# New orders on four engines in the attention rounds of a gated attention and expert block, and slots kept in PSUM

## The reference, cut to what matters

```
x = x + tanh(g0) * attn(layernorm(x), ctx)      # 16 heads of 16, window of 256:
                                                # softmax(q k^T + band) v, then the output projection
y = layernorm(x) * gamma + beta
probs = softmax(y @ Wr.T)                       # 8 experts, the top 2 of each token
slot  = rank of the token among those of its expert, kept if rank < 640
h = silu(gate(y)) * up(y);  out = h @ W3[e]     # per expert, 1024 hidden
x = x + tanh(g1) * sum of the two experts' outputs * their probs
```

## Time and profile before

| | us |
|---|---|
| median of 3 timed runs | 530.26 (529.48 to 530.85) |
| profiled execution, its time | 527.21 |
| its span | 525.3 |
| TensorE busy in it | 480.7 |
| VectorE busy | 352.1 |
| ScalarE busy | 295.5 |
| GpSimd busy | 189.1 |
| mean granted clock of TensorE | 0.967 |

### The profile page before, as it was taken

One profiled execution on the slowest core, in us unless ns is written; L12 is line 12 of the kernel. 1 busy time (PEld: TensorE's weight loads), 2 busy tenths in 40 slices (PEclk: granted clock), 3 DMA queues, 4 the chain that ended last, 5 costly groups with the idle time before them and its releaser, 6 DMA issues.

```text
span 525.3 us, 10673 instructions
## 1 busy us (share of the span) xinstructions
PE 480.7 (92%) x3566; PEld 443.5 (84%) x3588; DVE 352.1 (67%) x864; ACT 295.5 (56%) x747; POOL 189.1 (36%) x257
## 2 busy tenths in 40 slices
PE   4887999999999997489999999999999999999991
PEld 3666887878878775389899999999999999999991
DVE  5495879797798998658776764585834867534340
ACT  5776777777877773427564643464632737324130
POOL 8406573857768476600203020203032030310302
PEclk9999999999999997589999999999999999999997
DMA  5979413414142611273666551355541474200111
GB/s 163 255 177 283 81 19 63 83 52 91 56 90 55 210 51 48 71 225 125 193 211 181 145 175 17 73 186 138 175 95 22 130 191 133 31 11 11 16 15 20
DMA packets 41650, 57.34 MB, mean 109 GB/s; under 512 B 3721, under 2 KB 38576, under 8 KB 39552
## 3 DMA queue, kind: packets, MB, share of 16 engines
q1 hardware_dynamic: 35008, 48.49, 31.4%
q0 software_dynamic: 6144, 8.07, 9.1%
q10 hardware_dynamic: 448, 0.14, 0.2%
HBM read 36.24 MB, written 16.72 MB: 101 GB/s over the span
## 4 chain that ended last, share of the span: by engine, by line
PE 55%; DVE 2%; issue 2%; POOL 1%; DMA 1%; ACT 0%; POOLq 0%; DVEq 0%
PE bank L1485 18%; PE bank L1487 17%; PE bank L1486 17%; PE bank L1479 2%; DMA expert_rows<-xr,slotu 1%; PE bank L1413 1%; PE bank L1279 0%; POOL expert_rows L475 0%; POOL out_tokens L547 0%; PE bank L1271 0%; DVE pT L946 0%; DVE xr L842 0%; DVE xr L840 0%; DVE ysc L1181 0%; ACT xnT L585 0%
## 5 line engine op out<-in xcount | busy, mean ns | idle before, releaser
L547 POOL DMA_INDIRECT out_tokens<-ysc,rows x32 | 49.4, 1544 | 243.7 <-DVE ysc L1181 236.5
L1485 PE MATMUL bank<-bXh,wh 128*128 128x384 f32 (+1 forms) x384 | 122.0, 318 | 1.5 <-issue 1.2
L1487 PE MATMUL bank<-bXh,wl 128*128 128x384 f32 (+1 forms) x384 | 121.8, 317 | 0.0
L1486 PE MATMUL bank<-bXl,wh 128*128 128x384 f32 (+1 forms) x384 | 121.8, 317 | 0.0
L761 ACT ACTIVATE sil<-bank 128x384 f32<-128x384 f32 (+1 forms) x96 | 43.7, 456 | 126.6 <-PE bank L1487 126.5
L1160 DVE TENSOR_TENSOR hF<-sil,bank 128x384 f32<-128x384 f32 (+1 forms) x96 | 48.9, 509 | 76.1 <-ACT sil L761 76.1
L631 ACT ACTIVATE p<-bank,nm 128x128 f32<-128x128 f32 x256 | 73.5, 383 | 30.9 <-DVE nm L941 30.9
L1485 PE MATMUL bank<-wh,hH 128*128 128x256 f32 x256 | 73.8, 288 | 0.3 <-DVE ysc L1181 0.3
L1486 PEld LDWEIGHTS bank<-bXl,wh 128*128 128x128 f32 x384 | 72.7, 189 | 1.4 <-issue 1.4
L1485 PEld LDWEIGHTS bank<-bXh,wh 128*128 128x128 f32 x384 | 72.7, 189 | 0.5 <-issue 0.5
L1487 PEld LDWEIGHTS bank<-bXh,wl 128*128 128x128 f32 x384 | 72.6, 189 | 0.0
(11 more groups left out here) (144 smaller groups left out, 821.8 us busy)
## 6 DMA issues: line engine op xcount, KB each, us to landing
stage<-in_w12T SPq DMA_DIRECT2D x16, 1024.0 KB, 4.8
stage<-in_w3T SPq DMA_DIRECT2D x8, 1024.0 KB, 5.6
expert_rows<-padrow SPq DMA_DIRECT2D x8, 662.5 KB, 8.5
rows<-expert_rows SPq DMA_DIRECT2D x7, 662.5 KB, 4.3
kM<-k SPq DMA_DIRECT2D x62, 64.0 KB, 2.4
cT<-in_ctxT SPq DMA_DIRECT2D x8, 256.0 KB, 3.3
out_tokens<-x_all SPq DMA_DIRECT2D x8, 256.0 KB, 2.3
x_all<-in_x SPq DMA_DIRECT2D x2, 640.0 KB, 5.8
```

Of the source, the lines that this page charges most:

```text
L547: pool.indirect_dma_start(out=out, out_offset=bass.IndirectOffsetOnAxis(rows[par][:, c, D + E:ROW].bitcast(U32), 0), in_=ysc[par][:, c, :] ...
L1485: nc.tensor.matmul(out_ap, ah, bh, start=start, stop=False)
L1486: nc.tensor.matmul(out_ap, ah, bl, start=False, stop=False)
L1487: return nc.tensor.matmul(out_ap, al, bh, start=False, stop=stop)
```

## The change

ScalarE: the three zero fills inside round 0 move ahead of it; in g0 the copy of the turned head outputs moves to the front of g1, behind the exps of g0 and the copy of the inputs; the copy of the keys moves from g3 to g2, behind the exps, and the router's copy behind it; the first bf16 copy of the values (`values1`) moves from g7 to g0 of the next round, the second (`values2`) from g0 to g1. GpSimd: `values_rest` of round 1 stays in front, but `values_third` of round 1 moves behind the deviations, the bias and the first residual. VectorE: `low_probs` moves ahead of the head outputs in g1, g3, g5 and g7 and ahead of the maxima in g0; low keys go ahead of the maxima in g3; guard and inverse of the probabilities' sum move from g5 to g6, `gate_columns` from g6 to behind the slots in g7; one zero fill moves into g1 of round 0; the intermediate `slot` is written to a free part of the PSUM bank in place of SBUF. TensorE: the first turn of head outputs moves from the end of g0 into g1, between the scores and the probabilities, and waits for three slot steps in place of two (the bank is read one step longer); its projection moves behind the value matmuls of g1.

```diff
--- before.py
+++ after.py
@@ -129,7 +129,6 @@
         pick = sb(pa, "pick", [P, K, SB, E], F32)
         member = sb(pa, "member", [P, SEQS, E], BF16)
         late = sb(pa, "late", [P, SB, E], F32)
-        slot = sb(pa, "slot", [P, SB, E], F32)
         pslot = sb(pa, "pslot", [P, K, SB, E], F32)
         two_e = sb(pa, "two_e", [P, E], F32)
         many = sb(pa, "many", [P, E], F32)
@@ -503,7 +502,8 @@
                 pool.wait_ge(ld_x[s], 16)
             values_rest(0, 0)
             values_third(0, 0)
-            body(0, 0, False, False, True, True, True, None)
+            normalize_inputs(2)
+            values_rest(1, 1)
             rstd1(XCUT[2], SEQS)
             for s in range(2, len(XCUT) - 1):
                 pool.wait_ge(ld_x[s], 16)
@@ -511,6 +511,7 @@
             pool.wait_ge(gates_ok, 1)
             then(pool.tensor_scalar(tbo[:, :], bob[:, :], tg[:, 0:1], None, ALU.mult))
             residual(0, 0, False)
+            values_third(1, 1)
             body(1, 1, True, False, True, True, True, None)
             pool.wait_ge(ld_pad, 16 * (E + 1))
             body(2, 0, True, True, True, True, True, None)
@@ -640,33 +641,32 @@
             def body(n, par, prev1, prev2, cur, nxt):
                 for g in range(NG):
                     G = NG * n + g
-                    if g == 7 and nxt:
-                        values(n + 1, Xp)
-                        values1(n + 1, 1 - par)
+                    if g == 1 and prev1:
+                        output_columns(SB * (n - 1), Xo)
                     if (cur and g >= 2) or (prev1 and g < 2):
                         high_probs(G - 2, g % 2, not prev1 and g < 4)
                     if g == 0 and prev1:
-                        output_columns(SB * (n - 1), Xo)
-                    elif g == 2 and prev2:
-                        x2_columns(n - 2, Xo)
-                    elif g == 3 and nxt:
-                        keys(n + 1, Xp)
+                        values1(n, par)
+                    elif g == 7 and nxt:
+                        values(n + 1, Xp)
                     if cur:
                         exps(G, g, not prev1 and g < 2)
-                    if g == 0 and cur:
+                    if g == 0 and cur and not prev1:
                         values2(n, par)
                     if g == 0 and nxt:
                         input_columns(n + 1)
-                    if g in (1, 2) and cur and not prev1:
-                        zero_low_keys(2 * g - 1)
-                        if g == 1:
-                            zero_low_keys(2)
-                    elif g == 4 and prev2:
-                        exps_of_logits(n - 2)
+                    elif g == 1 and prev1:
+                        values2(n, par)
+                    elif g == 2 and nxt:
+                        keys(n + 1, Xp)
+                    if g == 2 and prev2:
+                        x2_columns(n - 2, Xo)
                     if g == 4 and prev1:
                         output_columns(SB * (n - 1) + 1, Xo)
                     if g == 4 and nxt:
                         queries(n + 1, 1 - par, Xp)
+                    if g == 4 and prev2:
+                        exps_of_logits(n - 2)
 
             def zero_low_keys(quarter):
                 act.activation(kM[1][:, 1, quarter * GH:(quarter + 1) * GH, :].rearrange("p h (a t) -> p (h a) t", t=P),
@@ -686,10 +686,13 @@
             for a in (2, 3):
                 r = slice(a * HD, (a + 1) * HD)
                 act.dma_start(kM[0][r, :, a:H:HR, :].bitcast(F32), k2[r, :, :, :].bitcast(F32)).then_inc(ld_km[0], 16)
+            zero_low_keys(1)
             act.wait_ge(bias_ok, 1)
             queries(0, 0, Q0)
+            zero_low_keys(2)
             values(0, Xo)
             values1(0, 0)
+            zero_low_keys(3)
             body(0, 0, False, False, True, True)
             body(1, 1, True, False, True, True)
             for i in range(1, NSB // 2 - 1):
@@ -925,9 +928,10 @@
                 if probs_between:
                     invert_sum(m, one)
                 dve.wait_ge(dve_rk, R_SLOT * s + 1)
-                dve.scalar_tensor_tensor(slot[:, a:b, :], late[:, a:b, :], LATE, rk, ALU.mult, ALU.add).then_inc(dve_rk, 1)
+                slot = bank[:, 2 * SB * E:2 * SB * E + (b - a) * E].rearrange("p (j e) -> p j e", e=E)
+                dve.scalar_tensor_tensor(slot, late[:, a:b, :], LATE, rk, ALU.mult, ALU.add).then_inc(dve_rk, 1)
                 dve.wait_ge(dve_rk, R_SLOT * s + 2)
-                dve.tensor_tensor(pslot[:, :, a:b, :], pick[:, :, a:b, :], slot[:, a:b, :].unsqueeze(1).to_broadcast([P, K, b - a, E]), ALU.mult)\
+                dve.tensor_tensor(pslot[:, :, a:b, :], pick[:, :, a:b, :], slot.unsqueeze(1).to_broadcast([P, K, b - a, E]), ALU.mult)\
                    .then_inc(dve_rk, 1)
                 if probs_between:
                     gate_columns(m, mpar, one)
@@ -994,30 +998,35 @@
                     routed = n - 2 if prev2 else None
                     if g in (2, 6) and prev1:
                         gated(n - 1, 1 - par, g // 4, Xo)
+                    if g == 3 and nxt:
+                        keys_low(n + 1, Xp)
                     if g == 4 and prev2:
                         clip_logits(routed, Xo)
+                    if g == 0 and prev1:
+                        low_probs(G - 2, g % 2)
+                    if cur:
+                        largest(G, g)
+                    if g == 4 and prev2:
+                        sort_logits(routed)
+                    elif g == 5 and nxt:
+                        queries_low(n + 1, 1 - par, Xp)
                     elif g == 6 and prev2:
                         sort_experts(routed)
-                    if cur:
-                        largest(G, g)
-                    if g == 3 and nxt:
-                        keys_low(n + 1, Xp)
-                    elif g == 5 and nxt:
-                        queries_low(n + 1, 1 - par, Xp)
-                    if g == 5 and prev2:
-                        sum_exps(routed)
-                    if g == 4 and prev2:
-                        sort_logits(routed)
-                    elif g == 5 and prev2:
-                        guard_sum(routed)
+                    if g == 1 and cur and not prev1:
+                        zero_keys(1, 0, 0)
+                    if g in (4, 6) and cur and not prev1:
+                        stats1(*XCUT[g // 2:g // 2 + 2])
+                    if (cur and g >= 2) or (prev1 and g == 1):
+                        low_probs(G - 2, g % 2)
                     if g == 4 and prev2:
                         shift_logits(routed)
                     elif g == 5 and prev2:
-                        invert_sum(routed)
+                        sum_exps(routed)
                     elif g == 6 and prev2:
                         pick_experts(routed)
-                    if g in (4, 6) and cur and not prev1:
-                        stats1(*XCUT[g // 2:g // 2 + 2])
+                        guard_sum(routed)
+                        members(routed)
+                        invert_sum(routed)
                     if g in (1, 3) and prev1:
                         k = 2 + g // 2
                         heads_out(HPS * (n - 1) + k, k, False)
@@ -1026,15 +1035,11 @@
                         k = (g - 5) // 2
                         heads_out(HPS * n + k, k, not prev1 and k == 0)
                         heads_scale(HPS * n + k, k, SB * n - 1 if prev1 else None)
-                    if (cur and g >= 2) or (prev1 and g < 2):
-                        low_probs(G - 2, g % 2)
-                    if g == 6 and prev2:
-                        members(routed)
-                        gate_columns(routed, par)
                     if g in (2, 6) and prev1:
                         stats2(n - 1, g // 4)
                     if g == 7 and prev2:
                         slots(routed, par, Xo)
+                        gate_columns(routed, par)
 
             def zero_keys(par, part, half):
                 dve.tensor_scalar(kM[par][:, part, half * H // 2:(half + 1) * H // 2, :].rearrange("p h (a t) -> p (h a) t", t=P),
@@ -1044,7 +1049,6 @@
             zero_keys(0, 0, 0)
             zero_keys(0, 0, 1)
             stats1(0, SB)
-            zero_keys(1, 0, 0)
             dve.wait_ge(pool_ln1, 1)
             normalize_inputs(0)
             dve.wait_ge(ld_b, 16)
@@ -1351,6 +1355,14 @@
                     G = NG * n + g
                     if cur:
                         scores(G, g, n, par, not prev1 and g < 2)
+                    if g == 1 and prev1:
+                        if prev3:
+                            pe.wait_ge(dve_rk, R_SLOT * (n - 3) + 3)
+                        elif prev2:
+                            pe.wait_ge(dve_x2, SB * (n - 1))
+                        else:
+                            pe.wait_ge(dve_bo, 1)
+                        output_columns(SB * (n - 1), Xo)
                     if (cur and g >= 2) or (prev1 and g < 2):
```

(16 more changed lines are left out.)

## The result

The changed kernel takes **531.78 us** (median of 20 runs, 529.10 to 534.44). In the same session the kernel before took 529.46 (20 runs, 527.48 to 531.89): ratio 1.0033, 95% interval 1.0016 to 1.0049. So the change costs 0.8 to 2.6 us: a small loss, with the middle of the interval (1.75 us) at the edge of the 1.6 us that the prediction took for no change. The profiled execution took 531.16, span 529.2. It lies 0.6 under its median, the one of before 2.25 under its own, and so the two profiles differ by 3.9 where the medians differ by 2.3.

A forecast was written before the change was run, and what follows sets the result against it. TensorE was taken to set the pace. Start -5.6, round 1 into 2 +2.6, rest of round 2 -0.25, later rounds +3.6, gate columns +0.5, last round +0.1 make +0.9: 530.26 becomes 531.2 us, range 527.6 to 535.5.

The forecast's parts named there:

- Start: Rounds 0 and 1: moved zero fills and GpSimd's new order bring round 1's queries from 53.27 to 47.7, -5.6 us.
- stall of 2.73 us: TensorE's wait in round 1 before 50.25, from GpSimd's order; forecast to go, with the clock's fall to 0.51 behind it.
- Period: Each later attention round: 24.1 us in place of 23.13, +0.97, with TensorE idle some 2.3 us in g1.
- The chain: VectorE from g5 maxima to g0 maxima 9.8 us, then exps and ScalarE's copies 2.7 us to the projection in g1.
- Round 2: Rest of round 2, after its g2 scores: forecast -0.25 us.
- Clock in g1: Rival, chance 0.18: idle 2.3 us before the projection lowers the clock; two or three rounds +4, all five +8; 535.2 us.
- a sign of being wrong: Wrong if period under 23.2, granted clock under 1 between 60 and 180 us, or gate columns of 0.5 us and more.
- The price I had set, 1.7: Cost in us of each fall of the granted clock in a round, in the clock rival.
- Slots in PSUM: VectorE's product of slots (L930), 0.73 us before, no longer waits for GpSimd: 0.55 us saved, between 0 and 0.57.
- surcharge: Skill's 62 extra cycles (0.065 us) for a PSUM source: saving 0.49, every round 0.06 longer; left out of the sum.
- Gate columns: VectorE behind the slots: +0.12 a round, +0.5 in all; rival, chance 0.14: held for a whole GpSimd operation, +3, 533.7 us.
- Last round: New idle replaces TensorE's 0.63 us wait for VectorE; VectorE's tail of statistics moves by +0.1 us.

The follow-up runs named there:

- run with maxima first: Changed kernel with VectorE's g0 maxima ahead of the low half of g6 again, as before: 526.05 us, ratio to before 0.9901 to 0.9945.
- run with the copy ahead of the exps: Changed kernel with ScalarE's copy of the turned head outputs in g0, ahead of the g0 exps: 525.93 us, ratio to before 0.9900 to 0.9944.
- run with low halves first: Kernel before plus new start and slots in PSUM, with VectorE's low halves ahead of head outputs in g1, g3, g5, g7: 529.74 us.

## Why the prediction was right, and where not

Forecast 531.2, measured 531.78. Between the two profiled executions, in stretches between TensorE's rows:

| stretch | forecast | measured |
|---|---|---|
| to the queries of round 1 | -5.6 | -4.54 |
| to the scores of g2, round 2 | +2.6 | +2.58 |
| to those of round 3 | +0.75 | +1.23 |
| to those of round 4 | +0.6 | +2.10 |
| to those of rounds 5 and 6 | +2.0 | +2.06 |
| gate columns | +0.5 | 0 |
| from there to the end | +0.1 | +0.47 |
| sum | +0.95 | +3.90 |

- **Start.** Forecast 47.7 for the queries of round 1, here 48.73. The first queries took 3.59 us where they took 1.97 before and in the run with maxima first. In that run the first scores start at 15.94 and the queries of round 1 at 47.73; in the changed kernel both come 1.0 later (16.93 and 48.73), so this one event is the whole miss. The single query matmuls took 0.63 us in place of 0.38. In the run with the copy ahead of the exps they took 0.63 too, with the granted clock at 0.50 from 12 to 14 us; here the clock column reads 1.00, so a fallen clock is likely but not shown. GpSimd's order did what it should (deviations 40.26, residual 43.27). With the stall of 2.73 us the fall behind it went too.
- **Period.** The chain was right link by link: VectorE from the g5 maxima to the g0 maxima 9.84 (forecast 9.8), from there to the projection 2.67 (2.7), g5 scores to projection 13.62 (13.6), period 24.16 (24.1), idle 2.08 ("some 2.3"). That the copy behind the exps and the low half ahead of the maxima carry it was shown: each one taken back gives 0.6 a round, both give 1.2.
- **Round 2** had none of the 0.25 that I gave it.
- **Clock in g1.** A rival in the forecast (0.18), and it came true in part (a clock under 1 between 60 and 180 us was also a sign of being wrong): one fall in the profiled execution, 1.65 us over two stretches (0.2 and 1.45 of the +1.23 and +2.10). The price I had set, 1.7, was right. The step that failed is that I made it all or nothing, and put it at nothing in the sum: at an idle so near to one that had brought a fall, one or two falls belonged in the sum.
- **Slots in PSUM.** 0.54 saved as taken from the earlier trace rows. The real worth is more: put back, 0.71 a round are lost, since the gate columns behind it are then held off too, besides two more clock falls. The surcharge that the Trainium skill gives for a PSUM source (VectorE: DVE Perf Modes, TRN2 errata, 62 cycles) is not seen: the product takes 0.19 us from PSUM, and 0.19 from SBUF where it isn't held off (before, at 209.05).
- **Gate columns** were not held off at all, forecast +0.12 a round. They began 0.1 before GpSimd's L459 ended and got through ahead of L461; in the run with slots in SBUF, begun inside L462, they were held for 0.42. The rule of the Trainium skill (SBUF — State Buffer, two separate sides) fits that run; it does not say which case the changed kernel is in, the rows do.
- **Last round.** +0.1 was too little: the projection idles 1.59 us there too, and from the scores of g2 in round 6 to those in round 7 it took 23.67 for 23.13, +0.54; the rest of the program gave 0.07 back.

What the forecast owes to luck: between the profiled executions it is 3 us off, between the medians 0.6 (from the 530.26 it started from) to 1.4 (from the 529.46 of 20 runs), since before's profile lay 2.25 under its median of 20 runs and that of the changed kernel only 0.6 under its own.

## What to carry to other kernels

Follow a buffer's chain across all engines around the loop: the period is the longest closed chain, and freeing time on one of its engines gives nothing unless that engine ends the chain. When a step is moved later on one engine, look at where its copy on the next engine goes: here the copy's new neighbours, not the move, cost the time. Parts of a change that each lose alone can win together, and the reverse: 6.5 us from the start were paid back by the order of two instructions, and undoing those two and then two waits behind them gave 520.1.

## What the runs showed of the hardware

- VectorE and GpSimd: with slots in SBUF, the product and the gate columns, which have two SBUF inputs and began during a GpSimd operation of 128x256 (L460, L462), ended only behind it (0.47 and 0.65 us for 0.19 and 0.23). With one input in PSUM the product did not wait (0.19). Nor did it, with two SBUF inputs, during GpSimd's operation of 128x1 (L447, 0.57 us): 0.19 there, at 209.05 in the kernel before.
- The same idle does not always bring the granted clock down, and the size of one idle does not decide it. With 2.08 us before the projection it fell in one of four rounds of the changed kernel; with slots in SBUF, where an idle of 0.6 us and only 0.36 us of work stand ahead of that one, in three of four; with 1.60 in none of four, and with 0.51 in none. In the run with low halves first, idles of 0.33 and 1.12 brought no fall in four cases, but 0.66 and 1.12, where round 7 begins, stand ahead of one (0.50 from 184 to 186 us). Each of these counts is from one profiled execution.
